# Second sweep of a two-layer graph kernel: the two layers' matmuls of a tile interleaved, from the sixth row panel on

## What is computed

```
def layer0(x, adj, weight):
    a_tilde = adj + eye
    d = rsqrt(sum(adj, axis=1) + 1e-6)
    return (d[:, None] * a_tilde * d[None, :]) @ (x @ weight)
def layer1(x, adj, ...):
    agg = adj @ x
    msg = relu(agg @ W_msg.T + b_msg)
    return gru_cell(msg, x)
x = layernorm(x + layer0(x, adj, weight))
x = layernorm(x + layer1(x, adj, ...))
```

## Time and profile before

| | us |
|---|---|
| median of three executions | 1787.47 |
| lowest, highest | 1787.13, 1789.02 |
| the profiled execution | 1789.12 |
| its span | 1787.3 |

### The profile page before, as it was taken

One profiled execution on the slowest core, in us unless ns is written; L12 is line 12 of the kernel. 1 busy time (PEld: TensorE's weight loads), 2 busy tenths in 40 slices (PEclk: granted clock), 3 DMA queues, 4 the chain that ended last, 5 costly groups with the idle time before them and its releaser, 6 DMA issues.

```text
span 1787.3 us, 17373 instructions
## 1 busy us (share of the span) xinstructions
PE 1647.3 (92%) x6413; PEld 1169.6 (65%) x6413; DVE 1478.2 (83%) x1555; ACT 772.6 (43%) x916; POOL 211.6 (12%) x127
## 2 busy tenths in 40 slices
PE   1088799997999999999999999999999999999997
PEld 0043344442444445888888888888788888888886
DVE  6988899999999975877666656656799999999997
ACT  0000021211112213545444444444587878787874
POOL 0000000000000001100000000000323232323231
PEclk7589999999999999999999999999999999999998
DMA  9999999999999983666666666655999899989993
GB/s 391 421 384 421 421 421 421 421 421 422 421 421 421 421 351 104 199 202 196 199 194 196 198 196 197 202 189 189 314 341 335 301 350 314 335 303 341 318 337 104
DMA packets 181396, 551.14 MB, mean 308 GB/s; under 512 B 13440, under 2 KB 14464, under 8 KB 148544
## 3 DMA queue, kind: packets, MB, share of 16 engines
q1 hardware_dynamic: 177824, 541.38, 81.4%
q0 software_dynamic: 2480, 8.13, 1.4%
q10 hardware_dynamic: 1008, 0.53, 0.1%
HBM read 545.79 MB, written 4.19 MB: 308 GB/s over the span
## 4 chain that ended last, share of the span: by engine, by line
PE 83%; DMA 11%; DVE 5%; ACT 0%; issue 0%; POOL 0%; SPq 0%; ACTq 0%; DVEq 0%; POOLq 0%
PE quad L469 21%; PE bank L526 13%; PE bank L528 13%; PE bank L527 13%; DMA kept<-adj_blocks 7%; PE quad L528 5%; PE quad L526 5%; PE quad L527 5%; DMA ring<-adj_blocks 4%; DVE colsum L959 3%; PE quad L603 1%; PE quad L604 1%; PE quad L605 1%; PE bank L452 1%; PE bank L443 1%; PE quad L495 1%
## 5 line engine op out<-in xcount | busy, mean ns | idle before, releaser
L986 DVE TENSOR_TENSOR lo<-ring,hi 128x2048 fp32r<-128x2048 f32 x106 | 242.9, 2291 | 210.8 <-ACT f L772 205.4
L526 PE MATMUL bank<-hi,x1s 128*128 128x512 f32 x1016 | 398.9, 393 | 1.0 <-DVE x1s L1049 1.0
L528 PE MATMUL bank<-hi,x1s 128*128 128x512 f32 x1016 | 395.9, 390 | 0.0
L527 PE MATMUL bank<-lo,x1s 128*128 128x512 f32 x816 | 317.8, 389 | 0.0
L761 ACT ACTIVATE hi<-ring 128x2048 fp32r<-128x2048 f32 x106 | 203.4, 1919 | 263.9 <-DMA ring<-adj_blocks 239.4
L469 PE MATMUL quad<-kept,feat 128*128 128x512 f32 x656 | 290.9, 595 | 20.6 <-DMA kept<-adj_blocks 20.6
L469 PEld LDWEIGHTS quad<-kept,feat 128*128 128x128 f32 x656 | 122.9, 190 | 179.9 <-issue 154.1
L732 ACT ACTIVATE part<-quad 128x512 f32<-128x512 f32 x72 | 39.1, 595 | 443.9 <-PE quad L469 443.9
L959 DVE TENSOR_TENSOR colsum<-colsum,kept 128x2048 f32<-128x2048 f32 x93 | 213.2, 2292 | 13.2 <-DMA kept<-adj_blocks 11.1
L528 PEld LDWEIGHTS bank<-hi,x1s 128*128 128x128 f32 x1016 | 190.7, 188 | 40.5
L526 PEld LDWEIGHTS bank<-hi,x1s 128*128 128x128 f32 x1016 | 190.8, 188 | 39.9 <-DVE x1s L1049 1.4
(11 more groups left out here) (163 smaller groups left out, 2202.3 us busy)
## 6 DMA issues: line engine op xcount, KB each, us to landing
ring<-adj_blocks SPq DMA_DIRECT2D x412, 512.0 KB, 5.3
kept<-adj_blocks SPq DMA_DIRECT2D x147, 1024.0 KB, 14.9
ring<-adj_blocks SPq DMA_DIRECT2D x56, 1024.0 KB, 14.9
pool<-adj_blocks SPq DMA_DIRECT2D x53, 1024.0 KB, 14.8
more<-adj_blocks SPq DMA_DIRECT2D x100, 512.0 KB, 5.7
xt<-x_t SPq DMA_DIRECT2D x8, 512.0 KB, 14.2
xin<-x POOLq DMA_DIRECT2D x16, 256.0 KB, 3.4
out<-y POOLq DMA_DIRECT2D x15, 256.0 KB, 5.3
```

Source lines behind the costliest of these rows:

```text
L526: pe.matmul(acc[:, :], fh, ah, start=start and c == 0, stop=False, skip_group_check=True)
L527: pe.matmul(acc[:, :], fh, al, start=False, stop=False, skip_group_check=True)
L528: mm = pe.matmul(acc[:, :], fl, ah, start=False, stop=stop and c == KC - 1, skip_group_check=True)
L986: ins = dve.tensor_tensor(flat(low(n)), flat(raw(slot_of2[n])), flat(hi[:, n % NHI]).bitcast(f32), ALU.subtract)
```

## The change

`APART` is the first tile of the sixth row panel of the second sweep, `start2[rows2[5]]` = 18. From tile 18 to tile 103 a new function `both_layers(n)` takes the place of `layer0(n)` and `layer1(n)`. It stands where `layer1(n)` stood, behind `turn(i)`. It issues the same 24 matmuls, with the two layers in turn: two neighbours have the same moving operand and different stationary operands, and write different banks. `first_done` is raised by the last matmul but one of the tile, `tile_done` by the last. The programs of the other engines are as they were.

```
+    APART = start2[rows2[5]]
...
+            def both_layers(n):
+
+                i, k = T2[n]
+                j = rows2.index(i)
+                pe.wait_ge(lo_ready, n + 1)
+                if n == start2[i]:
+                    pe.wait_ge(tall_ready, j - 1)
+                    pe.wait_ge(spilled, j - 1)
+                pe.wait_ge(x1_whole, norm_no[k] + 1)
+                begin, stop = n == start2[i], n == end2[i]
+                for c in range(KC):
+                    ah, al = hi[:, n % NHI, c, :], low(n)[:, c, :]
+                    fh, fl = f0[:, n % 2, c, 0, :], f0[:, n % 2, c, 1, :]
+                    xh, xl = x1s[:, k * KC + c, 0, :], x1s[:, k * KC + c, 1, :]
+                    first, second, last = acc0[j % 2], acc1[j % 2], stop and c == KC - 1
+                    pe.matmul(first[:, :], fh, ah, start=begin and c == 0, stop=False, skip_group_check=True)
+                    pe.matmul(second[:, :], xh, ah, start=begin and c == 0, stop=False, skip_group_check=True)
+                    pe.matmul(first[:, :], fh, al, start=False, stop=False, skip_group_check=True)
+                    pe.matmul(second[:, :], xh, al, start=False, stop=False, skip_group_check=True)
+                    mm0 = pe.matmul(first[:, :], fl, ah, start=False, stop=last, skip_group_check=True)
+                    mm1 = pe.matmul(second[:, :], xl, ah, start=False, stop=last, skip_group_check=True)
+                mm0.then_inc(first_done, 1)
+                mm1.then_inc(tile_done, 1)
...
             for n in range(1, NN - 2):
-                if 2 <= n < N2:
+                if 2 <= n < APART:
                     layer0(n)
                 i = normed_row(n, 1)
                 if i is not None:
                     turn(i)
-                if n < NN - 2:
+                if APART <= n < N2:
+                    both_layers(n)
+                elif n < NN - 2:
                     layer1(n)
```

## The result

The change makes the kernel slower: the median of four executions is 1839.1 us (1838.7 to 1840.1), against 1787.7 for the kernel before, a ratio of 1.028 with a 95% interval of 1.027 to 1.030. Forecast were 1834.7, and a range of 1818 to 1848. The profiled execution took 1840.1 us, its span is 1838.3.

A forecast was written before the change was run, and what follows sets the result against it. TensorE bounds the second sweep, so only matmul spacing and waits count. Turns of 33.5 and 1.7 us plus 12.0 for the clock make 47.2 us, added to 1787.5 for 1834.7 us; range 1818 to 1848.

The forecast's parts named there:

- Spacing: TensorE's matmuls in alternated tiles: alternating banks and sharing the moving operand leave 226.7 ns each, so 0 us.
- Turns of panels 8 to 1: Row ends in the second sweep: each turn loses its cover and waits for the sum, 4.19 us each, 33.5 us together.
- Turn of panel 9: Turn before tile 18: only the cover of tile 18's first layer is gone, a loss of 1.70 us.
- Turn of panel 0: Turn at tile 104: it never had a first layer behind it; at most 0.1 us added, taken as 0.
- Ordinary tiles and the later loads: Tiles between turns keep 1.8 us of cover, and third-sweep loads issued about 2.5 us later cost nothing: 0 us.
- The clock: TensorE's granted clock falls once at each of eight new holes, 1.5 us each, 12.0 us; range 0 to 28.8.
- the clock stays low longer at each hole: Rival for the second sweep's holes: each slow stretch is followed by another, giving 1851.5 us; chance 0.11.
- the prediction's own case: Uncovered turns plus one clock fall at each of eight holes: 1834.7 us, by itself 1828 to 1841; chance 0.61.
- The held clock: Rival for the second sweep: the waits at the turns come but the clock holds, 1822.7 us; chance 0.14.
- Sharing the operand: Rival on TensorE's alternated matmuls: a shared moving operand saves 13.4 ns per pair, 13.8 us, giving 1820.9; chance 0.08.
- the single bank: Rival on TensorE: one bank kept matmuls apart; alternating cuts spacing to 188 ns, saves 79.9 us, giving 1754.8; chance 0.02.
- the comparison of lengths: Clock at TensorE's holes: falls expected at holes longer than the 2.02 us wait before the one fall, none at 1.70.

The follow-up runs named there:

- the kernel with the filled holes: The change plus 17 matmuls into an unused bank ahead of the turn at the eight full holes; 1824.4 us, ratio 1.020.
- the first experiment: The change with alternation kept, but the turn of panels 9 to 1 issued behind the next tile; 1788.0 us, ratio 0.9997.
- the experiments with holes of 2.2 and 2.7 us idle: Against the change: 8 matmuls into an unused bank ahead of each of eight turns, 1832.3 us; turn behind the next tile's first chunk, 1819.8 us.

## Why the prediction was right, point by point

- **Spacing, 0 us.** Right: 5.44 us for a tile before and after, and the kernel with the covered turn at a ratio of 0.9997. The Trainium skill's page "TensorE: Matmul & The Clock Gate", section "Back-to-back issue gap", puts the isolated gap of 512 columns at N / 2.4 + 2.5, about 216 ns. The 22.7 us of the prediction follow from that page's measured 215.7, which stands in other sections of it; the rows stay at 226.7 ns.
- **Turns of panels 8 to 1, 8 x 4.19 us.** Right to 0.01 us: 4.41 less 0.23, eight times, 4.02 idle in the records as the text had asked. Both halves of the argument, the turn's new place and the later release, were needed: the place alone is 1.69 per turn (the experiment without alternation).
- **Turn of panel 9, 1.70.** Measured 1.69, and no fall of the clock.
- **Turn of panel 0, 0.** Right: it waits 0.56 us in the changed kernel, 0.57 before.
- **Ordinary tiles and the later loads, 0.** Right; the waits name `tall` alone as new, and the spans differ by no more than the second sweep does.
- **The clock, 12.0.** The mechanism was right, one fall at each full hole and none at the short one; the size was low. It is 16.1. A single fall costs 1.6, or 1.4 where part of it lies in the hole, near the 1.5 taken. The term that was mis-sized is the number of stretches: three of the eight falls were twice as long. They cost 2.7 on average and not the 3.6 of the upper end, as part of each lay in the hole. The rival "the clock stays low longer at each hole" was thus true at three holes in eight. It accounts for the 4 of the 51.4 us that the forecast of 47.2 lacks. The range of the prediction's own case was also added up too wide: 1787.5 + 35.2 + 8 x 1.8 and two more is 1839.1, not 1841, and the measured median lies at that edge.
- **The rivals.** The held clock would have been 1822.7; the kernel with the filled holes is just that case, and gave 1824.4, 35.5 over its baseline where 35.2 had been forecast. Sharing the operand and the single bank are both excluded by the first experiment.

One loose step of the prediction is the comparison of lengths: a fall at each new hole because these are longer than the 2.02 us ahead of the one fall, and none at 1.70 because that is shorter. Nine such short holes in one kernel had none, and eight long ones had eight, so both conclusions hold. But the experiments with holes of 2.2 and 2.7 us idle show that the comparison is no rule, and the trace of the kernel before already said so. Its timeline and its windows view have a longer wait 21 us earlier, with the clock at 1.00; the last line is the windows view of the changed kernel behind the same wait, there 2.47 us:

```profile
169.39 3.70 PE L469 MATMUL quad<-kept,feat 128*128 128x512 f32 x8 [2.48 <-DMA kept<-adj_blocks]
...
168.00:173.00 5.00, 3.61 (x8) 1.44 (x8) 4.74 (x4) 0.00 (x0) 0.00 (x0) 1.00 1.01 419
...
170.40:173.90 3.50, 3.50 (x5) 1.35 (x4) 3.43 (x3) 0.00 (x0) 0.00 (x0) 0.51 1.02 424
```

Another wait of 2.48 us, at 411.73, had no fall either, so of three waits over 2 us in the middle of that trace one had a fall. In the changed kernel's execution all three had one. That every full hole would drop the clock was thus forecast from the one case that did, and is in part luck.

No version beats the kernel before. The alternation with a covered turn equals it.

## What to carry to other kernels

Ask of every step in a tuned stream what it was covered by, not only what it costs: four transposes, 0.6 us together, made TensorE wait for nothing as long as 24 matmuls stood over the chain of two other engines that leads to them, and 4.2 us per turn once those were gone. An interleaving moves two things at once, the place of the steps around it and the moment at which its results are released; write down for both who waits. And where a hole on TensorE can't be avoided, its price is the hole and the clock behind it; covering it even with useless matmuls got back 16 us of 51 here, moving one instruction on VectorE got back 45.

## What the runs showed of the hardware that was not expected

- In the second sweep a fall of the granted clock comes in two sizes, 3.4 and 6.8 us, though TensorE had dense work ahead of it and behind it in both cases. In the four profiles with eight holes of 4.0 us idle every hole had a fall (32 of 32), and of these 11 were double. With the five of the kernel changed from panel 5 on it is 37 and 12, and the double ones are those that began 0.71 us or more ahead of the turn.
- Of eight equal holes with 2.7 us idle four dropped the clock, of eight with 2.2 five, of seventeen with 1.3 to 1.6 us idle none.
- Neighbouring matmuls that share the stationary operand, the moving operand, the bank or none of these stand in the same 226.7 ns from start to start, as the mean over a tile, for 128x512 in fp32r with a weight load each. By the rows here nothing about operands or banks is to be gained at this shape.
